# Two-layer attention kernel on one core: projections in halves, several side operations one position later, and both score pairs of a step issued under one wait

## What is computed

```python
# layer 1: causal attention, 16 heads of width 8
Q, K = rope(x @ wq.T), rope(x @ wk.T);  V = x @ wv.T
x = layernorm(x + softmax(causal(Q K^T / sqrt(8))) V @ wo.T)
# layer 2: pre-norm attention without a mask, then routed experts
h = layernorm(x, ln1);  q, k, v = split(h @ w_qkv)
y = x + softmax(q k^T / sqrt(8)) v @ w_proj
z = layernorm(y, ln2);  e = argmax(z @ gate_w + gate_b)      # one of 8 experts per row
y = y + gelu(z @ w1[e]) @ w2[e]
out = layernorm(x + y)
```

## Time and profile before

| | |
|---|---|
| median of 3 runs | 914.34 us |
| the profiled execution: its time / its span | 915.0 us / 913.3 us |
| PE, PE weight loads | 90%, 41% busy |
| ACT | 85% busy (777.6 us) |
| DVE, POOL | 36%, 24% busy |
| mean granted TensorE clock | 0.953 of full speed |
| ACT `probs<-ps`, line 864 | 832 instructions, 732.6 us busy, 52.7 us idle before them |

### The profile page before, as it was taken

How to read it: one execution, slowest core, us unless ns; L and a number is a source line. 1 busy time by engine, 2 the same in 40 slices (tenths; PEclk the granted TensorE clock), 3 DMA queues, 4 the chain that set the end, 5 groups by cost and what they waited for, 6 DMA issues and landing times.

```text
span 913.3 us, 24231 instructions
## 1 busy us (share of the span) xinstructions
PE 819.6 (90%) x9924; PEld 372.1 (41%) x9936; DVE 328.7 (36%) x948; ACT 777.6 (85%) x913; POOL 223.1 (24%) x359
## 2 busy tenths in 40 slices
PE   6689899999999999999999999999999999996271
PEld 3344344444444444444343444443444434443231
DVE  3711644410431005330042333264332463334753
ACT  1568789899999999999999999998999999994460
POOL 4732131111100110000003333323234132343333
PEclk9789999999999999999999999999999999998586
DMA  8976120202020250720201000201000010001101
GB/s 264 271 222 197 48 78 17 94 2 48 1 94 1 70 118 2 249 76 2 47 2 32 1 2 4 76 10 33 2 3 19 14 42 2 2 3 31 38 5 41
DMA packets 34357, 51.60 MB, mean 57 GB/s; under 512 B 4032, under 2 KB 14656, under 8 KB 34240
## 3 DMA queue, kind: packets, MB, share of 16 engines
q1 hardware_dynamic: 32704, 46.30, 17.7%
q0 software_dynamic: 1536, 3.67, 1.3%
HBM read 29.12 MB, written 20.84 MB: 55 GB/s over the span
## 4 chain that ended last, share of the span: by engine, by line
PE 58%; issue 21%; DVE 8%; ACT 5%; DMA 3%; POOL 3%; POOLq 2%; ACTq 0%; SPq 0%; DVEq 0%
PE ps L479 54%; ACT probs L864 3%; PE ps L484 2%; POOLq L999 2%; PE ps L738 1%; DMA early_late<-z_sorted 1%; POOL parts L1006 1%; DMA z_sorted<-z_rows,slot_numbers 1%; DVE ln_newton L1068 1%; POOL z_sorted L977 1%; DVE squares_blockdiag L1353 0%; DVE ln_newton L1067 0%; DMA early_late<-in_sin 0%; DVE ln_newton L1066 0%; DVE squares_blockdiag L1352 0%
## 5 line engine op out<-in xcount | busy, mean ns | idle before, releaser
L864 ACT ACTIVATE probs<-ps 128x1024 f32<-128x1024 f32 (+3 forms) x832 | 732.6, 1014 | 52.7 <-PE ps L479 51.0
L479 PE MATMUL ps<-probs,values 128*9 128x256 f32 (+1 forms) x6528 | 429.3, 376 | 4.3 <-POOL probs L972 1.8
L479 PE MATMUL ps<-query_rows,key_rows 32*128 32x512 f32 (+3 forms) x1664 | 289.8, 486 | 16.2 <-ACT probs L864 12.0
L479 PEld LDWEIGHTS ps<-probs,values 128*9 128x9 f32 x6528 | 143.6, 90 | 184.4 <-issue 95.2
L479 PEld LDWEIGHTS ps<-query_rows,key_rows 32*128 32x128 f32 x1664 | 121.6, 183 | 195.2 <-issue 95.3
L972 POOL TENSOR_SCALAR_AFFINE_SELECT probs<-probs 128x256 f32<-128x256 f32 x128 | 53.1, 421 | 238.9 <-ACT probs L864 236.0
L1013 POOL COPY parts<-early_late 128x512 f32 x63 | 42.7, 716 | 147.5 <-PE ps L479 147.4
L977 POOL DMA_INDIRECT z_sorted<-z_rows,slot_numbers x16 | 15.8, 990 | 213.9 <-DVE slot_numbers L1341 204.4
L1209 DVE COPY q_rotated<-ps 128x512 f32<-128x512 f32 x30 | 20.7, 690 | 129.6 <-PE ps L479 129.6
L1006 POOL COPY parts<-parts 128x512 f32 x72 | 45.4, 671 | 29.6 <-PE ps L479 27.8
L1221 DVE RECIPROCAL recip<-ps 128x16 f32<-128x16 f32 x32 | 8.2, 256 | 82.1 <-PE ps L484 82.1
(11 more groups left out here) (171 smaller groups left out, 573.6 us busy)
## 6 DMA issues: line engine op xcount, KB each, us to landing
k_scratch<-parts SPq DMA_DIRECT2D x16, 512.0 KB, 3.8
q_scratch<-parts SPq DMA_DIRECT2D x16, 512.0 KB, 5.1
query_rows<-q_scratch SPq DMA_DIRECT2D x32, 256.0 KB, 5.3
key_rows<-k_scratch SPq DMA_DIRECT2D x20, 256.0 KB, 4.9
key_rows<-k_scratch SPq DMA_DIRECT2D x16, 192.0 KB, 4.5
parts<-in_w SPq DMA_DIRECT2D x1, 2048.0 KB, 8.3
early_late<-in_w SPq DMA_DIRECT2D x8, 256.0 KB, 7.1
early_late<-z_sorted SPq DMA_DIRECT2D x4, 384.0 KB, 3.2
```

What stands on the lines that cost most here:

```text
L479: return nc.tensor.matmul(out, l, r, start=start, stop=stop, skip_group_check=True)
L864: nc.scalar.activation(Pr[:, t % KEPT, 2 * p:2 * p + 2, lo:BLK], score_banks(t, p)[:, :, lo:BLK], ACT.Exp, bias=-SHIFT[r["a"]], scale=SCAL ...
```

## The change

- `POST_AT` 7: `post_project` is two halves at positions 6 and 7 (before: whole at 6). `GATE_AT` 12: `m_gate` is two halves at 11 and 12 (before: whole at 11). `m_ranks` stays at 13.
- The three projections of the second attention are two halves each, at the position before their place and at their place. Blocks 1 and 4 of `PREP_AT` move some places by one.
- Sorted rows and the first rounds of the experts are one position later; the first `gelu` is asked for one position earlier before each turn (`due(at - 2)`).
- VectorE: `between` hooks let events be made inside `bound` (before its wait for the small matmul) and inside `layernorm` (after the first of three Newton turns); `split2` asks for events once more after the keys are rounded.
- `scores` in the second attention waits once, for the exponential that frees the second pair's slot, and issues all four matmuls.

```diff
-UP_AT = (25, 31, 38, 44, 50, 57)
-TURN_AT = (29, 36, 42, 48, 54, 61)
-DOWN_AT = (33, 40, 46, 53, 59, 63)
-SORTED_AT = (22, 23)
+UP_AT = (26, 32, 38, 44, 50, 57)
+TURN_AT = (30, 36, 42, 48, 54, 61)
+DOWN_AT = (34, 40, 46, 53, 59, 63)
+SORTED_AT = (23, 24)
...
-    (14, 16, 18, 20, 22, 23, (24, 26, 28, 30)),
+    (14, 16, 18, 21, 23, 24, (25, 26, 29, 30)),
     (14, 17, 19, 21, 23, 25, (28, 32, 36, 40)),
     (14, 17, 20, 22, 24, 26, (28, 32, 36, 40)),
-    (13, 15, 17, 18, 20, 22, (25, 26, 29, 30)),
+    (13, 15, 17, 19, 21, 23, (25, 26, 29, 30)),
 )
+POST_TURN_AT, POST_AT, GATE_AT = 5, 7, 12
...
-            def project2_queries(b):
+            def project2_queries(b, n):
                 s = A[2]
-                turn_taken()
-                pe.wait_ge(s["k_taken"], b + 1)
-                mm(ps7, wqkv[:, 0:D], hT[:, :]).then_inc(s["q_proj"], 1)
+                c = slice(n * BLK // 2, (n + 1) * BLK // 2)
+                if n == 0:
+                    turn_taken()
+                    pe.wait_ge(s["k_taken"], b + 1)
+                last = mm(ps7[:, c], wqkv[:, 0:D], hT[:, c])
+                if n == 1:
+                    last.then_inc(s["q_proj"], 1)
...
                 r, t = step["r"], step["t"]
+                together = r["a"] == 2
                 for p in range(2):
-                    if 2 * t + p:
+                    if together and p == 0:
+                        pe.wait_ge(exp, 2 * t + 1)
+                    elif not together and 2 * t + p:
                         pe.wait_ge(exp, 2 * t + p)
...
-                freed = [(6, post_x, n)]
+                freed = [(POST_AT, post_x, n)]
...
-                todo = {5: [lambda: post_turn(n - 1)], 6: [lambda: post_project(n - 1)]}
+                todo = {POST_TURN_AT: [lambda: post_turn(n - 1)]}
+                for m in range(2):
+                    todo[POST_AT - 1 + m] = [lambda m=m: post_project(n - 1, (m,))]
                 if a == 2 and qb:
                     b = qb - 1
-                    todo.update({10: [lambda: m_turn(b)], 11: [lambda: m_gate(b)], 13: [lambda: m_ranks(b)]})
+                    todo.update({10: [lambda: m_turn(b)], 13: [lambda: m_ranks(b)]})
+                    for m in range(2):
+                        todo[GATE_AT - 1 + m] = [lambda m=m: m_gate(b, (m,))]
...
-                rsqrt(y, v, h, t, 3)
+                rsqrt(y, v, h, t, 1)
+                between()
+                newton(y, h, t, 2)
...
                 ts(kdg[:, :], ident[0:H, 0:H], u, 1.03, ALU.mult, ALU.mult).then_inc(diag_set, 1)
+                between()
                 dve.wait_ge(bound_mm, a)
...
-                link(layernorm(xb, xb))
+                link(layernorm(xb, xb, lambda: due(10)))
                 due(11)
...
                 link(copy(rounded(k3, b), ka[:, :]))
+                due(at[1] + 1)
                 if b == 0:
...
-                        due(at - 1)
+                        due(at - 2)
                         gelu(b, r)
...
-                    bound(1)
+                    bound(1, lambda: due(BOUND1_AT))
...
-                    due(10)
                     rows_to_h(n - 1, due)
```

More of the change, by code:

```diff
@@ L670, in post_turn, with post_project @@
                 turned(ps7, lambda i: att[:, i, :]).then_inc(post_t, 1)
-            def post_project(n):
-                pe.wait_ge(post_e, n + 1)
-                for i in range(TB):
+            def post_project(n, halves=(0, 1)):
+                if 0 in halves:
+                    pe.wait_ge(post_e, n + 1)
+                for i in (i for m in halves for i in (2 * m, 2 * m + 1)):
                     last = mm(ps[:, 7, i * D:(i + 1) * D], attT[:, i * P:(i + 1) * P], (wo if n < NB else wproj)[:, :])
-                last.then_inc(post_p, 1)
+                if 1 in halves:
+                    last.then_inc(post_p, 1)
             def z_turn(b):
@@ L687, in m_turn, with m_gate @@
                 turned(ps7, lambda i: zb[:, i, :]).then_inc(m_zT, 1)
-            def m_gate(b):
-                pe.wait_ge(m_h, b + 1)
-                for i in range(TB):
+            def m_gate(b, halves=(0, 1)):
+                if 0 in halves:
+                    pe.wait_ge(m_h, b + 1)
+                for i in (i for m in halves for i in (2 * m, 2 * m + 1)):
                     last = mm(ps[:, 7, i * E:(i + 1) * E], hT[:, i * P:(i + 1) * P], gw[:, :])
-                last.then_inc(m_g, 1)
+                if 1 in halves:
+                    last.then_inc(m_g, 1)
             def m_ranks(b):
@@ L811, in side_of @@
                 b, at = n - 1, PREP_AT[n - 1]
-                ops = (z_turn, project2_keys, project2_queries, project2_values, lambda b: key_norms(2, b), lambda b: query_norms(2, b))
-                for p, f in zip(at, ops):
-                    todo[p] = [lambda f=f: f(b)]
+                for p, f in zip(at[1:4], (project2_keys, project2_queries, project2_values)):
+                    for m in range(2):
+                        todo[p - 1 + m] = [lambda f=f, m=m: f(b, m)]
+                todo.update({at[0]: [lambda: z_turn(b)], at[4]: [lambda: key_norms(2, b)], at[5]: [lambda: query_norms(2, b)]})
                 for i, p in enumerate(at[6]):
@@ L1064, in rsqrt, with newton @@
                 link(ts(h, v, -0.5, None, ALU.mult))
+                newton(y, h, t, turns)
+            def newton(y, h, t, turns):
                 for _ in range(turns):
@@ L1068, in rsqrt, with layernorm @@
                     link(nc.vector.scalar_tensor_tensor(out=y, in0=t, scalar=1.5, in1=y, op0=ALU.add, op1=ALU.mult))
-            def layernorm(dst, src):
+            def layernorm(dst, src, between=lambda: None):
                 for i in range(TB):
@@ L1074, in layernorm, with normalize @@
                 link(ins)
-                return normalize(dst, src)
-            def normalize(dst, src):
+                return normalize(dst, src, between)
+            def normalize(dst, src, between=lambda: None):
                 for i in range(TB):
@@ L1130, in take_query_norms, with bound @@
                     link(tt(qmx[:, 0:1], qmx[:, 0:1], qmx[:, 1:2], ALU.max))
-            def bound(a):
+            def bound(a, between=lambda: None):
                 u, y, h, t = (bw[:, m:m + 1] for m in range(4))
```

24 lines of the change are left out of this document (15 added, 9 removed).

## The result

| | before | after |
|---|---|---|
| median of 8 runs each (range), us | 913.94 (910.02 to 917.52) | 920.45 (914.84 to 926.81) |
| ratio after / before, 95% interval | | 1.0067 [1.0038, 1.0097] |
| profiled execution: time / span, us | 915.0 / 913.3 | 921.1 / 919.3 |
| mean granted clock in it | 0.953 | 0.945 |

The forecast was 910.0 us with a range of 904 to 918. The time lies above the range, on the side to which it gave a chance of 0.16, and not for the reason named there.

What follows compares the result with a forecast made beforehand. ScalarE's exponentials bound the kernel, with 52.7 us idle before them, mostly ended by TensorE's scores. Terms -3.1 - 2.6 + 0.5 + 0.1 - 1.5 + 5.4 - 4.2 - 0.6 + 1.6 = -4.4, from 914.3 to 910.0 us; range 904 to 918.

Steps and rivals of the forecast that it cites:

- The pairs together, 0: Attention 2's scores: one wait for both pairs costs nothing; the Trainium skill's reading would give some 4 us less.
- With the stall gone I expect the full 2.4 GHz: Attention 1, block 0: earlier copy saves 1.8 us, full clock another 1.3 before the scores of 58.68; together -3.1.
- Two of three: Attention 2, blocks 1 to 3: two new clock falls behind the idle before the ranks, 0.8 us each, +1.6.
- I expect these three to stay: Attention 2, position 30 of blocks 1 to 3: old clock falls behind the tanh remain, each costing 1.43 us.
- the first rival: The clock holds: neither the new falls (1.6) nor the old three (3 x 1.43) are paid; 904 us, chance 0.17.
- Block 2, a new wait of 1.3: Attention 1, block 2: values wait for the sums' copy behind the later layernorm chain, +1.3; block sum +0.5.
- Halves elsewhere, -0.4 a pair: Halved projections overrun by 0.1: `post_project` -0.4 in each later block; attention 2's block 0, -1.5 in all.
- Ranks, +5.4: Attention 2, blocks 1 to 3: the later gate makes TensorE idle 1.8 us before the ranks, +1.8 each.
- Sorted rows, -4.2: Attention 2, blocks 1 to 3: one position later, TensorE's 4.3 us wait for their DMA goes.
- the second rival: The sorted rows' wait moves along, so the 4.2 us come back; no change, 914 us, chance 0.17.
- The gelu, -0.6: Gelu before the turn of position 36 asked for ahead of `norm`: -0.3 in each of two blocks.
- The third rival: Clock falls in plain steps, where TensorE idles 0.42 of every 1.83 us; slower, 927 us, chance 0.16.

Runs made afterwards that it cites:

- experiments 1 and 7: Score pairs under one wait, alone on the kernel before: 0.9991; changed kernel with pairs apart: 1.0063; also with whole projections and later block 3 query projection: 0.9903.
- experiment 4: Kernel before with VectorE's three earlier copies and sorted rows and first rounds one position later, nothing in halves, pairs apart: ratio 0.9928 [0.9904, 0.9951].

## Why the prediction was wrong, by its own steps

The waits that the halves set were found and sized rightly, all three. Their price was not, since the clock fell behind them and elsewhere where no fall was counted, and the halves gave back half of what was booked for them or less.

- *The pairs together, 0*: right, by the kernels of experiments 1 and 7. The four matmuls do run side by side, but the -4 us that the prediction read from it didn't come.
- *The clock*: this is the step that failed. "With the stall gone I expect the full 2.4 GHz" (block 0): up to position 8 the block was 3.04 us shorter, as the term says, and then the clock fell at 60.5 us instead of 55.4 and took 1.97 back. It is a matter of the execution: six of fourteen had no such fall, and with 2.2 to 2.8 us less than before came near the term. In block 1 the falls of 91.2 and 121.9 us took 2.8 us: without them it took 58.54, 3.0 less than the kernel before, which had a fall of its own there (75.9), and 1.9 less than two kernels of the old order without one (60.43). No fall was counted behind the wait in block 2 (159.5, 183.3). Blocks 0 to 2 of attention 1 hold 7.4 of the 10.5 us between forecast and profile. "A first attention that isn't 5 us shorter" was the prediction's own sign of a broken sum: it was 2.9 us longer.
- *The clock in attention 2*: "Two of three" new falls behind the ranks: all three came, at 1.5, 0.8 and 0.8 us (positions 15 and 16), and ten of twelve over all kernels with the wait. "I expect these three to stay" (position 30): all three were gone, -4.8 us, which is what the first rival had put forward; but with the copies alone, whose order there is the old one, they were gone too, so that is not shown to be the change's doing.
- *Block 2, a new wait of 1.3*: the mechanism and the wait were right (1.16 us), the price was not: 3.5 us for the block, 3.65 by the run that takes it away (2.5 where only one fall came).
- *Halves elsewhere, -0.4 a pair*: too much. The gap goes (-0.44 at position 7), but both split steps overrun, and the next one gives +0.24, so -0.2 is left. Where one gap of 0.57 us stood there are two, of 0.12 and 0.13, and a further break of the row of exponentials. In attention 2's block 0 the projections' three gaps (1.30 us in all) became six, of 0.10 to 0.13 each (0.68), where the prediction had 0.2 in all. So attention 2's block 0 won 0.3 us instead of 1.5. The prediction took a half for 0.54 us, 0.1 over the free 0.42. In the timeline of the changed kernel, one half of the out projection starts at 595.89 and the next scores at 596.53: a half holds TensorE for 0.64, and two such steps start 2.06 us apart, not 1.93.
- *Block 3, first query half behind `norm`, +1.3*: right, a gap of 1.34 us in the profile.
- *Ranks, +5.4*: the wait was right, its price too small. Up to position 14 the three blocks lost 2.60, 2.10 and 2.09 us where 1.8 each was forecast, and 9.8 together with the clock behind them, instead of 7.0; removing the wait gave 1.0% of the run.
- *Sorted rows, -4.2*: right at their place, -4.7 by the profile; that refutes the second rival, whose wait moves along. *The gelu, -0.6*: wrong. The gap at position 37 shrank in two blocks (0.33 and 0.35 us to 0.13 with what stands at 36), but gaps of 0.23, 0.23 and 0.51 us came at position 35 and one of 0.21 at 38 in the last block, and positions 32 to 38 of the three blocks are 1.2 us longer. The kernel of experiment 4 has the gaps at 35 too, so they come with the shift. Its total shows no gain from the shift that can be told from the noise.
- *Blocks 1 to 3 of attention 2*: that they came out at +2.0 where +2.2 was forecast is luck. The ranks and their falls cost 2.8 us more, the gelu and the shift 1.8 more, and the vanished falls gave 4.8.
- *The third rival*, falls in plain steps: refuted by the window above. That the kernel came out slower is not its doing.

How much of the loss is clock? Over the 216 runs of all kernels I took, for each run, the time at the lower level as 2 x (1 - mean clock) x span, and compared it with the run's time among runs of one kernel on one chip: 0.36 us longer for each us at 1.2 GHz, correlation 0.88. The falls of block 2 give the like, 1.1 to 1.5 us for 3.4. The kernel after has on average 98.0 us there, that before about 85: 13 x 0.36 = 4.7 of the 6.5 us. This is a correlation within kernels, carried over to a difference between two, and no run fixed the clock alone; the waits of ranks and copy and their falls come and go together. What is shown is that taking away the two waits and the third one in block 3 brings all of it and another 0.9%, as much as the copies bring alone. So the shift, the halves, the gelu and the pairs together have no gain that any ratio shows. Where the 4.2 us promised for the sorted rows went is explained only in part, by the gaps at position 35 and the further breaks between exponentials.

## What to carry to other kernels

When a projection is split over two steps, look at the consumer of its *second* half: every chain behind it starts a step later, and if its reader on TensorE stays at its place, the split turns into a wait that costs more than the overrun it smooths. Move the reader in the same edit; that alone turned +0.7% into -0.3%, and with the copy and the query projection moved too, into -0.9%. That is no more than the copies gave by themselves, so here splitting was at best free: each split gap breaks the row of exponentials once more.

Price a new wait of TensorE in a dense stretch at two to three times its length (1.16 us came with 2.5 or 3.65, three of 1.7 to 1.8 with 9.8 together), since the lower clock mostly came behind it, and don't book a removed fall as a gain: it may come back a few us on, in one execution and not in the next. For the same reason compare ratios of many runs, and a block of one profile only with that block in other kernels of the same order.

For this kernel, take the three earlier copies: -0.8% by themselves, at 0.9917 [0.9887, 0.9946]. The changed kernel with the two projections whole and the later query projection has 0.9902 [0.9874, 0.9930] and, on a second chip, 0.9918 [0.9890, 0.9945], which isn't shown to be better.

## What the runs showed of the hardware beyond expectation

- A fall of the clock went with much less than its length: about 0.36 us for each us at half the clock, where ScalarE sets the pace. Falls that come and go also spread the times: eight runs of the changed kernel range over 1.3% (914.84 to 926.81), and the shorter ones have the higher mean clock (0.954 at 914.84, 0.937 at 926.81).
- Exponentials in a row overlap by 0.15 us each, and a gap between them costs about 0.1 us more than it shows as idle time (the estimate under the result).
- Regular short idle times did not lower the clock here: at 0.34 us in every 1.83 (16.56 busy of 20 us) it stayed at 1.00. The Trainium skill ("TensorE: Matmul & The Clock Gate", "A second HAM failure mode: psum-queue depth-cycling") describes a clock that oscillates under micro-idle times between groups of matmuls; the plain steps of this trace don't show it. The falls stood behind stretches with single long waits (1.61, 1.88 and 2.51 busy of 3.40 us), yet another with 2.28 busy, right behind the tanh where a fall had stood before, was not followed by one:

```profile
511.00:514.40 3.40, 2.28 (x36) 0.72 (x28) 2.64 (x4) 2.92 (x5) 2.79 (x4) 1.00 0.00 0
514.40:517.80 3.40, 2.52 (x36) 1.06 (x40) 0.30 (x1) 3.40 (x5) 0.00 (x0) 1.00 0.00 0
```

  Before, 2.36 busy in a like stretch was followed by one. So busy share over a stretch that I choose doesn't tell whether a fall comes; what does is open.
